# Moving every second query product from VectorE to GpSimd in the last third of a linear-attention layer

## What is computed

```python
qkv = x @ W_qkv
q, k, v = split into heads
q = relu(q @ W_f + b_f); k = relu(k @ W_f + b_f)
kv = einsum('bhnd,bhne->bhde', k, v)
out = einsum('bhnd,bhde->bhne', q, kv)
normalizer = einsum('bhnd,bhd->bhn', q, k.sum(axis=2))
out = out / (normalizer[..., None] + 1e-06)
x = layernorm(x + (out @ W_out + b_out))
x = layernorm(x + ffn(x))
```

## Time and profile before

| | us |
|---|---|
| median of 3 runs | 359.92 (359.8 to 361.12) |
| profiled execution | 359.96 |
| its span, first to last instruction | 358.2 |
| mean granted TensorE clock in it | 0.981 of full speed |

### The profile page before, as it was taken

How to read it: one execution, slowest core, us unless ns; L and a number is a source line. 1 busy time by engine, 2 the same in 40 slices (tenths; PEclk the granted TensorE clock), 3 DMA queues, 4 the chain that set the end, 5 groups by cost and what they waited for, 6 DMA issues and landing times.

```text
span 358.2 us, 5159 instructions
## 1 busy us (share of the span) xinstructions
PE 323.6 (90%) x1841; PEld 228.1 (64%) x1841; DVE 238.8 (67%) x489; ACT 173.1 (48%) x289; POOL 75.8 (21%) x77
## 2 busy tenths in 40 slices
PE   4898999999699999999999999999997988978980
PEld 3765667776477767676767677666685656545550
DVE  2635999974968676667625864488368577688553
ACT  2532336434537444575455555554645655344340
POOL 3079749940000000101000110011011011011211
PEclk9999999999899999999999999999999998998998
DMA  6981353829303700910190009200830560570011
GB/s 187 271 257 60 117 176 119 288 72 206 86 2 90 150 0 6 204 31 3 44 197 0 0 6 205 62 1 6 190 74 2 132 138 2 129 169 0 0 51 39
DMA packets 25090, 33.74 MB, mean 94 GB/s; under 512 B 3656, under 2 KB 13928, under 8 KB 25064
## 3 DMA queue, kind: packets, MB, share of 16 engines
q1 hardware_dynamic: 24904, 33.38, 37.0%
q10 hardware_dynamic: 160, 0.03, 0.0%
HBM read 31.04 MB, written 2.36 MB: 93 GB/s over the span
## 4 chain that ended last, share of the span: by engine, by line
PE 69%; DVE 13%; DMA 7%; POOL 3%; issue 3%; ACT 2%; SPq 2%; POOLq 0%; DVEq 0%; ACTq 0%
PE ring L502 25%; PE kx_ps L574 13%; PE attn_ps L502 9%; PE ring L665 5%; PE ring L594 4%; PE ring L554 4%; PE desk L511 3%; DMA x<-_L_ffn_down_weights_dram 3%; DVE qn L1022 2%; DVE stats L1031 2%; POOL rstd L481 2%; PE desk L608 2%; DMA recips<-recip_rows 2%; PE desk L583 2%; DMA xs<-in_L_attn_x_dram 2%
## 5 line engine op out<-in xcount | busy, mean ns | idle before, releaser
L787 ACT ACTIVATE q<-ring,bf_col 128x512 f32<-128x512 f32 x64 | 43.9, 686 | 52.7 <-PE ring L502 52.3
L574 PE MATMUL kx_ps<-k,xs 128*128 128x512 f32 x128 | 60.2, 592 | 0.8 <-ACT k L780 0.8
L478 POOL TENSOR_TENSOR var_eps<-mean_var,ln_eps 128x4 f32<-128x4 f32 x16 | 7.4, 465 | 243.3 <-DVE mean_var L1035 243.3
L780 ACT ACTIVATE k<-ring 128x512 f32<-128x512 f32 x64 | 38.3, 598 | 33.6 <-PE ring L554 33.3
L773 ACT ACTIVATE qn_h<-qn 128x512 fp32r<-128x512 f32 x64 | 39.7, 627 | 28.2 <-DVE qn L1022 28.2
L923 DVE TENSOR_TENSOR qn_l<-qn,qn_h 128x512 fp32r<-128x512 f32 x64 | 42.8, 679 | 14.1 <-ACT qn_h L773 13.4
L1022 DVE TENSOR_TENSOR qn<-q,recips 128x512 f32<-128x512 f32 x64 | 42.3, 701 | 4.0 <-DMA recips<-recip_rows 4.0
L470 POOL TENSOR_TENSOR y<-hid,y_up 128x512 f32<-128x512 f32 x18 | 33.6, 1887 | 22.8 <-DMA hid<-in_L_ffn_up_weights_dram 22.1
L574 PEld LDWEIGHTS kx_ps<-k,xs 128*128 128x128 f32 x128 | 24.1, 189 | 19.2 <-issue 16.5
L502 PE MATMUL ring<-xT_h,wq_h 128*128 128x512 f32 x64 | 35.7, 558 | 0.0
L502 PE MATMUL attn_ps<-qn_h,m_h 128*128 128x512 f32 x64 | 28.2, 441 | 7.3 <-DVE y_dn L945 2.9
(11 more groups left out here) (130 smaller groups left out, 527.0 us busy)
## 6 DMA issues: line engine op xcount, KB each, us to landing
recips<-recip_rows SPq DMA_DIRECT2D x32, 512.0 KB, 7.2
hid<-in_L_ffn_up_weights_dram SPq DMA_DIRECT2D x9, 512.0 KB, 4.9
x<-_L_ffn_down_weights_dram SPq DMA_DIRECT2D x9, 512.0 KB, 4.8
xs<-in_L_attn_x_dram SPq DMA_DIRECT2D x4, 512.0 KB, 6.1
out_dram<-y SPq DMA_DIRECT2D x8, 256.0 KB, 7.3
q<-in_L_attn_W_qkv_dram SPq DMA_DIRECT2D x2, 512.0 KB, 7.9
q<-in_L_attn_W_qkv_dram SPq DMA_DIRECT2D x2, 256.0 KB, 3.3
q<-in_L_attn_W_out_dram SPq DMA_DIRECT2D x2, 256.0 KB, 8.4
```

What stands on the lines that cost most here:

```text
L574: t_.matmul(kx_ps[half], xs[b % XBUF][:, t, :], k[kt % KRING][:, half * CH:(half + 1) * CH], start=t == 0, stop=t == TILES - 1).then_inc(s ...
L780: a_.activation(k[kt % KRING][:, half * CH:(half + 1) * CH], bank(("k", kt, half))[:, :], ACT.Relu).then_inc(s_taken, 1)
L787: a_.activation(q[:, i % QRING, :], bank(("q", i))[:, :], ACT.Relu, bias=bf_col[:, :])\
```

## The change

From step 36 on (`SHARED` = 2 x (32 - 4 - 10) = 36, slot 28), VectorE makes only the even steps' products, and GpSimd the odd ones: 37, 39, ... 63, fourteen of them. GpSimd's product stands in its program ahead of that slot's `rstd_of`, and waits for what VectorE's waited for. It counts on a semaphore of its own; `normalised` turns "product a is there" into a wait on one or both semaphores for ScalarE's high part, for the reuse of a query buffer and for SP's refill of `recips`. The arithmetic is the same.

```diff
+    SHARED = 2 * (ALLT - FIRST - SPREAD_AT)
...
-        s_qn = sem("qn_done")
+        s_qn = sem("qn_done_by_dve")
+        s_qnp = sem("qn_done_by_pool")
...
+        def normalised(eng, a):
+
+            made = a + 1
+            if made <= SHARED:
+                eng.wait_ge(s_qn, made)
+            else:
+                eng.wait_ge(s_qn, SHARED + (made - SHARED + 1) // 2)
+                if made - SHARED >= 2:
+                    eng.wait_ge(s_qnp, (made - SHARED) // 2)
...
                     if g >= 2:
-                        sp.wait_ge(s_qn, RC * (g - 1))
+                        normalised(sp, RC * (g - 1) - 1)
...
+                for a in spreads(s)[1:]:
+                    if a >= SHARED:
+                        pool.wait_ge(s_rc[a // RC % 2], 32 * (a // RC // 2 + 1))
+                        pool.wait_ge(s_qnh, a - 1)
+                        pool.wait_ge(s_qnl, a - 1)
+                        g.tensor_tensor(qn[:, a % 2, :], q[:, a % QRING, :], recips[:, a // RC % 2, a % RC, :],
+                                        ALU.mult).then_inc(s_qnp, 1)
                 if s in ATT_T_SLOT:
                     rstd_of(0, ATT_T_SLOT[s])
...
                 if i >= QRING:
-                    act.wait_ge(s_qn, i - QRING + 1)
+                    normalised(act, i - QRING)
...
             def qn_hi(a):
-                act.wait_ge(s_qn, a + 1)
+                normalised(act, a)
...
                 for a in spreads(s):
-                    normalise_q(a)
+                    if a < SHARED or a % 2 == 0:
+                        normalise_q(a)
```

## The result

The changed kernel takes 365.65 us (median of 4 executions, 363.79 to 366.42) against 359.86 before: a ratio of 1.0139, 95% interval 1.010 to 1.0178, so 1.4% slower. A second set on another occasion gave 1.0112 (1.0087 to 1.0137). The profiled execution took 363.79 us, 3.8 more than that of before, with a span of 361.9.

A forecast was written before the change was run, and what follows sets the result against it. In slots 28 to 41 the chain from 261 us on was taken to lie no longer on PE but through VectorE, ScalarE and GpSimd; -0.6 - 0.1 + 0.8 + 0.2 + 0.3 + 0.1 = +0.7 gave 360.6 us, range 359.0 to 365.6.

The forecast's parts named there:

- rival 1: Slots 31, 32, 35, 38, 40: GpSimd's product holds up the norm's end, 1.0 us each, 364.6 us; chance 33%.
- The failed step: Norm's end beside GpSimd's small addition and power at 339.16 us, 1.09 us: taken to show no contention, bound 0.2 us.
- the term of 0.2 us a slot: Slots behind a layer norm: GpSimd's product holds up VectorE's first product, which ends at R + 1.92 instead of R + 1.75.
- the 0.3 of slot 34: Slot 34: both engines released by the same landing; with VectorE first, its low part ends 0.3 us later.
- slot 32's reciprocal: Slot 32: without the second product the reciprocal, and everything behind it up to slot 34, starts 0.61 us earlier: -0.6.
- slot 38's copy: Slot 38: ScalarE's second high part, ahead of the attention-sum copy, no longer waits 0.08 us for its product: -0.1.
- slot 39: Slot 39: GpSimd's product follows VectorE's first product, and the low part ends less than 0.1 us later: +0.1.
- odd products that ScalarE never had to wait for: Slots behind a norm: GpSimd's product is ready when ScalarE asks, after its other high part and a ReLU; no cost.
- SP not held: SP's refill waits for products 43 and 47 were claimed to be met in time, so SP isn't held.
- Rival 3: The clock: longer idle times of PE call up more half-clock stretches; chance 10%.
- Rival 2: A gain: the engines hardly meet, GpSimd being stepped over, -0.6 - 0.1, 359.2 us; chance 12%.

The follow-up runs named there:

- the run with one instruction: Changed kernel with the norm's end as one 128x512 instruction instead of four of 128x128: 0.55 us undisturbed, 1.50 beside GpSimd's product.
- the removal alone: Kernel before, with the fourteen odd query products from slot 28 on made by nobody: ratio 0.9949, 359.12 us against 360.33.
- the run with the addition alone: Kernel before, VectorE making all products and GpSimd making the fourteen odd ones again into an unread tile: ratio 1.0225, 368.4 us.

## Why the prediction was right or wrong, point by point

The ratio of 1.0139 lies inside the range (365.6 / 359.9 = 1.0158); the median itself, 365.65 us, stands at its upper end of 365.6. The range was wide enough to hold two opposite answers to one question, and the likelier answer was the wrong one: I forecast 360.6 us at 45%, and rival 1 (364.6 us, 33%) came about. That the range held is owed to the rival that stood in it, and not to the sum. What failed is one step.

- **The failed step** is "So the nearest row says that the norm's end doesn't contend, and the sum goes by it". The row was true and the wrong witness. GpSimd's instructions there handle 4 elements a partition; they left the norm's end undisturbed, as they do in the changed kernel's own tail (1.08 us at 342.88), while a product of 512 holds one of the four for 0.94 to 0.97 us, and the term of 0.2 us a slot measured about 0.95. A small partner shows nothing on how long a large one holds. Nothing else in the trace before put a large GpSimd instruction beside a `tensor_scalar`, so the 33% of rival 1 was my estimate. The norm's end does go faster for its size than a product (0.55 us for 128x512 in the run with one instruction, against 0.68), but no run shows that this is why it is held up.
- **The size of rival 1.** It had 0.94, rounded to 1.0, per slot. Measured in the five slots: 0.97, 0.93, 1.26 less the 0.3 of slot 34, about 0.95 and 0.95. Its sum of +4.7 stands against +4.9 up to slot 40 (of which 0.25 arose ahead of slot 30), and against +5.8 and +3.8 in the two sets, whose difference from it no run explains.
- **Its mechanism in detail was wrong in all but one slot.** In five of six slots GpSimd doesn't get in between the four; it is first. I had it start 0.08 us behind rstd, from the gap between two dependent GpSimd instructions. With its waits long met it starts 0.03 us before the end of rstd. Only at 317.48 us, where it waits for a DMA, did it come about as described. The price is the same either way: the four take 2.06 to 2.08 us in the five slots and 2.09 in the sixth. That rival 1's price fits so well is in part luck, since it was worked out for the second instruction.
- **The terms that held**, from the trace after: slot 32's reciprocal 0.60 us earlier (-0.6); slot 38's copy 1.77 instead of 1.86 us behind the first product (-0.1); slot 34 with VectorE first, the low part at 1.00 instead of 0.69 us (+0.3); slot 39, 2.31 instead of 2.25 us up to the addition (+0.1); odd products that ScalarE never had to wait for on the chain; SP not held. The +0.2 per slot for a held *product* was never called up, because the held norm's end moved the product out of GpSimd's way; from slot 30 on all VectorE products took at most 693 ns.
- **Rival 3 (a half-clock stretch of PE more or fewer).** The chances and the range use a worth for such a stretch on the path that no run shows. What the traces show is a granted clock of 0.51 from 297.0 to 300.5 us and, where the stretch at 327.7 us is missing, 1.1 us less from slot 40 to slot 43's addition (8.93 us in the changed kernel and 8.94 in the removal alone, instead of 10.07).
- **Rival 2 (a gain)** needed that the two hardly meet; the run with the addition alone is 2.3% slower.
- **The chances.** "Slower" came about at 44%, against 51% for "same" and 5% for "faster": the 45% behind "same" rested on the failed step.

## What to carry to other kernels

Before moving work to GpSimd, list what VectorE runs in the same microsecond, and sort it by what it lost here. Beside a GpSimd product a pair of two-tensor products from SBUF took 2.39 us instead of 1.29, a low part 1.00 instead of 0.69, and the SBUF-to-SBUF `tensor_scalar` of fp32 stood still for 0.95 us of the product's 1.28, while a PSUM-input addition (0.69 us) and the statistics (0.87 us) kept their times. The costly place was directly behind the GpSimd instruction that VectorE waited for, where GpSimd's product went first in five of six slots; one added wait brought the ratio from 1.0139 to 1.0016. And look first at the engine's own idle times on the chain: putting the next product into a 1.18 us wait shortened the slot distance by 1.07 us and the kernel by 1.2%, and no second engine was needed for it.

## What the runs showed that I had not expected

- What collided depended on the kind of instruction on both engines: VectorE's products ran at 693 ns or less beside GpSimd fills, and up to 1.8 us beside GpSimd products; one `tensor_scalar` of the norm's end, 343 ns undisturbed, took up to 1191 ns beside the fills and 1314 beside the product.
- A GpSimd product whose waits were met started before the rstd in front of it is shown as ended (267.49 against 267.52 us), and so ahead of VectorE, which that rstd's semaphore released (267.56). It did so in five of six slots.
- Fourteen GpSimd products that nobody uses, 19.7 us on an engine with almost nothing else to do there, cost 8 us of the whole.
